# Sum over heads once per four batches, and two recurrences with gates made at eviction, a setup at the start and exponents summed by a scan

## The reference, cut to what matters

```python
# L0_attn (RWKV): k, v, r are projections; k of this reference is constant in time
#   the state's maximum pp, numerator aa and denominator bb run over 32 tokens:
#   q = max(pp, tf); e1 = exp(pp - q); e2 = exp(tf - q)
#   y = sigmoid(r) * (e1 * aa + e2 * v) / (e1 * bb + e2 + 1e-6);  out = y @ out_w.T

# L1, L2, L3 cross attention: 16 heads of depth 8, 257 keys per sequence
scores = jnp.einsum('bhqd,bhkd->bhqk', qh, kh) / sqrt(8)      # + mask or log weights
attn = softmax(scores)
out = einsum('bhqk,bhkd->bhqd', attn, vh) -> concat heads @ dense_w.T + dense_b

# L2_attn (RG-LRU)
gate_x = sigmoid(block_linear(x, ig_w, ig_b)); gate_a = sigmoid(block_linear(x, ag_w, ag_b))
log_a = -8.0 * gate_a * softplus(a_param)
a = exp(log_a); a2 = exp(2.0 * log_a)
normed_x = x * gate_x * sqrt(maximum(1.0 - a2, 1e-07))
p = cumprod(a, axis=1); p_prefix = maximum(concatenate([ones, p[:, :-1]]), 1e-07)
h = p_prefix * cumsum(normed_x / p_prefix, axis=1)
```

## Time and profile before

| | us |
|---|---|
| median of 3 runs (3683.45 to 3694.7) | 3692.14 |
| profiled execution | 3689.13 |
| its span | 3687.2 |
| busy in it: PE 2674.5, DVE 2416.8, ACT 1807.5, POOL 1662.8 | |
| first block, to the first norm | 16.2 |
| norm and recurrence of rwkv | 221.0 to 323.7 |
| norm and recurrence of rglru | 2174.3 to 2331.3 |
| cross attentions x1, x2, x3 with their norms | 808 to 1330, 1640 to 2174, 2740 to 3245 |

### The profile page before, as it was taken

How to read it: one execution, slowest core, us unless ns; L and a number is a source line. 1 busy time by engine, 2 the same in 40 slices (tenths; PEclk the granted TensorE clock), 3 DMA queues, 4 the chain that set the end, 5 groups by cost and what they waited for, 6 DMA issues and landing times. The chain is left out here.

```text
span 3687.2 us, 98216 instructions
## 1 busy us (share of the span) xinstructions
PE 2674.5 (73%) x27184; PEld 2116.8 (57%) x27185; DVE 2416.8 (66%) x8780; ACT 1807.5 (49%) x5569; POOL 1662.8 (45%) x1768
## 2 busy tenths in 40 slices
PE   5962577739999979757999970367748999978562
PEld 3741466626777669645777740256636777747552
DVE  5965711148999947646999976551148999969615
ACT  2451033328888723325888865213327777734221
POOL 2620055517777700004777740015526777736162
PEclk9975588969999979878999985559979999979665
DMA  2003043421111100201333300214434544400122
GB/s 79 1 0 96 25 118 111 117 75 40 37 37 36 28 7 0 109 0 52 72 74 72 74 25 0 55 42 116 112 87 113 110 111 111 101 1 1 35 88 69
DMA packets 209738, 224.95 MB, mean 61 GB/s; under 512 B 29651, under 2 KB 177619, under 8 KB 208948
## 3 DMA queue, kind: packets, MB, share of 16 engines
q1 hardware_dynamic: 196948, 197.56, 20.5%
q0 software_dynamic: 12672, 25.98, 2.8%
HBM read 201.68 MB, written 21.76 MB: 61 GB/s over the span
## 5 line engine op out<-in xcount | busy, mean ns | idle before, releaser
L1765 ACT ACTIVATE sx<-sx,nm 128x257 f32<-128x257 f32 x1536 | 770.5, 505 | 264.2 <-DVE nm L1809 264.2
L1680 POOL TENSOR_TENSOR sx<-sx,rs 128x1028 f32<-128x1028 f32 x384 | 731.9, 1906 | 372.0 <-DVE rs L1815 372.0
L1809 DVE CUSTOM_DVE_ANT_0 sx<-bank,rows 128x257 f32<-128x257 f32 x1024 | 393.1, 422 | 53.7 <-PE bank L1755 35.5
L247 POOL TENSOR_TENSOR rstd<-var,nhalf 128x16 f32<-128x16 f32 x24 | 69.7, 2905 | 775.3 <-DVE var L264 775.3
L1443 ACT ACTIVATE hT<-bank,B 128x128 f32<-128x128 f32 x714 | 206.0, 368 | 432.2 <-PE bank L1411 260.8
L1469 DVE TENSOR_TENSOR yb<-bank,b2s 128x128 f32<-128x128 f32 x159 | 46.4, 292 | 429.6 <-remote 230.5
L1765 ACT ACTIVATION_READ_ACCUMULATOR sx<-sx,nm 128x1 f32 x1536 | 290.3, 189 | 0.0
L1424 PE MATMUL bank<-W,hT 128*128 x1428 | 236.2, 313 | 60.6 <-ACT hT L1443 44.1
L1755 PE MATMUL bank<-kT,qb 32*128 32x257 f32 x3072 | 275.7, 428 | 6.0 <-DVE nm L1809 6.0
L1744 PE MATMUL bank<-pt,vs 128*32 128x128 f32 x6144 | 247.5, 278 | 40.1 <-ACT pt L1774 34.7
L1826 DVE COPY pt<-bank 128x512 f32<-128x512 f32 x384 | 263.6, 687 | 3.3 <-PE bank L1700 2.9
(11 more groups left out here) (391 smaller groups left out, 5924.8 us busy)
## 6 DMA issues: line engine op xcount, KB each, us to landing
ct<-in_ctxT SPq DMA_DIRECT2D x384, 128.5 KB
W<-in_L_w SPq DMA_DIRECT2D x159, 256.0 KB
rows<-rows_x SPq DMA_DIRECT2D x256, 128.5 KB
keep<-rows_keep SPq DMA_DIRECT2D x128, 128.5 KB
yg<-copy_outs SPq DMA_DIRECT2D x40, 256.0 KB
token_rows<-XN SPq DMA_DIRECT2D x24, 256.0 KB, 2.3
W<-in_L_w SPq DMA_DIRECT2D x39, 128.0 KB
wu<-in_up_w SPq DMA_DIRECT2D x1, 4608.0 KB, 14.1
```

The lines of the kernel that those rows point to most:

```text
L1680: pool.tensor_tensor(sx[:, j, :, 0:KEYS], sx[:, j, :, 0:KEYS], rs[:, j, :].unsqueeze(2).to_broadcast([P, 4, KEYS]), ALU.mult).then_inc(p_r ...
L1765: ins = act.activation(sx[:, j, h, 0:KEYS], sx[:, j, h, 0:KEYS], ACT.Exp, bias=nm[:, j, h:h + 1], scale=-1.0, accum_out=sm[:, j, h:h + 1])
L1809: dve.tensor_tensor_reduce(sx[:, j, h, 0:KEYS], B[h][:, 0:KEYS], add, -1.0, 3.0e38, ALU.add, ALU.min, nm[:, j, h:h + 1]).then_inc(s_summed ...
```

## The change

In the first block the vectors V are loaded first, with a semaphore of their own, and ACT and DVE compute there what rwkv computed at its beginning, and rglru's three scales (lru). These values live in tiles of their own (RW, decay, recur, lru). In norm, jobs named in `gates` are evicted by ACT with Sigmoid; for rglru both jobs are, and NA is 2. The loops of both recurrences are written out, and the add to X moves behind the next group's work. rglru sums the gate's values by a scan (CS, shifted by a column, set to zero where a sequence begins) and takes p and its inverse ip as two exponentials of that sum; the Exp, Ln and Exp for the root run as three passes over all groups, the last one merged with p and ip; GpSimd makes the product of gate and input. In xattn `a` has four batches in two buffers with a fifth slot for the last key's part, the sum over heads is one reduction of 4 x 32 x 5 values per four batches, and the matmul with the output weights and the add come one step later.

The core of the diff; the loops written out and the moved setup are cut:

```diff
+                sp.dma_start(V[:], T["vecs"]).then_inc(vecs_loaded.sem, 16)
...
+                st_ = Steps(act, sig, "act_step")
+                act.wait_ge(*vecs_loaded(1))
+                st_.link(act.activation(lru[:, 0:1], v("a_param"), ACT.Abs))
+                st_.link(act.activation(lru[:, 0:1], lru[:, 0:1], ACT.Exp, scale=-1.0))
+                act.activation(lru[:, 0:1], lru[:, 0:1], ACT.Ln, bias=1.0).then_inc(c_done.sem, 1)
+                act.wait_ge(*a_done(1))
...
+                dve.wait_ge(*vecs_loaded(1))
+                st_.link(dve.tensor_scalar(relu_td[:], relu_td[:], td, None, ALU.max))
...
+                st_.count(dve.tensor_copy(recur[:], ex[:, 3, :]))
+
+                st_.link(dve.tensor_copy(decay[:, :, 1:S], ex[:, 2, 0:S - 1].unsqueeze(1).to_broadcast([P, 16, S - 1])))
+
+                dve.wait_ge(*c_done(1))
+                st_.link(dve.tensor_scalar(lru[:, 3:4], lru[:, 3:4], v("a_param"), None, ALU.max))
...
-                NA = (5, 6, 5, 6)[len(jobs)]
+                NA = (5, 6, 5, 6)[len(jobs)] if len(gates) < 2 else 2
...
+                        for j in (0, 1):
...
+                                act.wait_ge(*psum[j](g + 1))
+                                act.activation(to[:, g * GW:(g + 1) * GW], B[2 + 2 * j + g % 2][:],
+                                               ACT.Sigmoid if j in gates else ACT.Identity, bias=bias).then_inc(done[j].sem, 1)
...
+                            st_.link(dve.tensor_tensor(ub[:, :, 1:S], vg[:, :, 0:S - 1], per_batch(recur[:, 0:S - 1], S - 1), ALU.mult))
...
+                            dve.tensor_tensor(y[:, q], y[:, q], RT[:, g * GW:(g + 1) * GW].rearrange("p (b s) -> p b s", s=S), ALU.mult)\
+                                .then_inc(scan_ready.sem, 1)
+                        g = k - 1
+                        if g >= 0:
+                            dve.wait_ge(*y_psum(g + 1))
+                            xg = X[:, g * GT:(g + 1) * GT, :]
+                            dve.tensor_tensor(xg, xg, B[g % 2][:].rearrange("p (t d) -> p t d", t=GT), ALU.add).then_inc(x_added.sem, 1)
...
+                        pool.tensor_tensor(GX[:, tok(g)], GX[:, tok(g)], XNT[:, tok(g)], ALU.mult).then_inc(gx_ready.sem, 1)
...
+                    for g in range(GROUPS):
+                        act.activation(A2[:, tok(g)], gate_a[:, tok(g)], ACT.Exp, scale=lru[:, 1:2]).then_inc(a2_ready.sem, 1)
...
+                        act.activation(A2[:, tok(g)], A2[:, tok(g)], ACT.Ln, scale=-1.0).then_inc(log_ready.sem, 1)
+                    act.wait_ge(*log_ready(GROUPS))
+                    for g in range(GROUPS):
+                        act.activation(A2[:, tok(g)], A2[:, tok(g)], ACT.Exp, scale=0.5).then_inc(root_ready.sem, 1)
+                        act.wait_ge(*cs_ready(g + 1))
+                        act.wait_ge(*scan_ready(g - 1))
+                        act.wait_ge(*y_psum(g - 1))
+                        act.activation(ip[:, g % 2, :], CS[:, tok(g)], ACT.Exp, scale=lru[:, 2:3])
+                        act.activation(p[:, g % 2, :], CS[:, tok(g)], ACT.Exp, scale=lru[:, 0:1]).then_inc(p_ready.sem, 1)
...
+                        dve.tensor_tensor_scan(CS[:, tok(g)], GA[:, tok(g)], keeps, 0.0, ALU.add, ALU.mult).then_inc(cs_ready.sem, 1)
+                        dve.wait_ge(*a2_ready(g + 1))
+
+                        dve.tensor_scalar(A2[:, tok(g)], A2[:, tok(g)], 1.0, -1e-7, ALU.subtract, ALU.min).then_inc(less_ready.sem, 1)
...
+                            st_.link(dve.tensor_tensor(GX[:, tok(g)], GX[:, tok(g)], A2[:, tok(g)], ALU.mult))
+                            dve.wait_ge(*p_ready(g + 1))
+
+                            st_.link(dve.scalar_tensor_tensor(out=GX[:, tok(g)], in0=ip[:, q, :], scalar=1e7, in1=GX[:, tok(g)],
+                                                              op0=ALU.min, op1=ALU.mult))
+                            st_.link(dve.tensor_tensor_scan(A2[:, tok(g)], keeps, GX[:, tok(g)], 0.0, ALU.mult, ALU.add))
+                            dve.scalar_tensor_tensor(out=p[:, q, :], in0=p[:, q, :], scalar=1e-7, in1=A2[:, tok(g)],
+                                                     op0=ALU.max, op1=ALU.mult).then_inc(scan_ready.sem, 1)
...
-                a = sb2("a", [P, 2, P])
+                a = sb2("a", [P, 2, 4, 5, S])
...
+                        if r_ % 4 == 3 and ok(x - 11):
+                            pe.wait_ge(*o_ready((x - 11) // 4 + 1 if isinstance(x, int) else i * (U // 4) + (r_ - 11) // 4 + 1))
...
+                        if r_ % 4 == 3 and ok(x - 11):
...
+                            dve.wait_ge(*a_ready(4 * (tl + 1)))
+                            dve.wait_ge(*pl_ready(tl + 1))
+                            dve.wait_ge(*y_psum(tl))
+                            dve.tensor_reduce(oT[:].rearrange("p (b s) -> p b s", b=4), a[:, tq].rearrange("p b j s -> p b s j"),
+                                              AX.X, ALU.add).then_inc(o_ready.sem, 1)
+                        b, q, tq = x - 5, (r_ - 5) % 4, (r_ - 5) % 8 // 4
...
-                            dve.wait_ge(*o_ready(4 * (tl + 1)))
-                            for k in range(4):
-                                to = oT[:, k * S:(k + 1) * S]
-                                ins = dve.scalar_tensor_tensor(out=to, in0=B[7][:, k * S:(k + 1) * S], scalar=VL[:, bass.ds(tl * 4 + k, 1)],
-                                                               in1=to, op0=ALU.mult, op1=ALU.add)
-                            ins.then_inc(pl_ready.sem, 1)
+                            dve.tensor_tensor(a[:, tq, :, 4, :], B[7][:, 0:P].rearrange("p (b s) -> p b s", b=4),
```

More of the change, by code:

```diff
@@ L208, in _ @@
                 sp.wait_ge(*loaded(2))
-        def norm(add_back=False, XN=None, fetch=None, jobs=()):
+            @block.scalar
+            def _(act):
+                st_ = Steps(act, sig, "act_step")
[4 more added lines that the diff above has]
+                act.wait_ge(*a_done(1))
+                act.activation(ex[:], ex[:], ACT.Exp).then_inc(b_done.sem, 1)
+                st_.close()
@@ L281, in _ @@
                         for j in (0, 2):
-                            if j < len(jobs):
+                            if j < len(jobs) and j not in gates:
                                 to, wt, frm, bias, scale = jobs[j]
@@ L538, in rwkv @@
                 VT, RT = sb2("VT", [P, TILES * P]), sb2("RT", [P, TILES * P])
[L539 to L546, removed]
+                norm(jobs=[(VT, w("a0_v"), XNT, v("zero"), 1.0), (RT, w("a0_r"), XNT, v("zero"), 1.0)], gates=(1,))
                 ub = sb2("ub", [P, 16, S])
@@ L608, in _ @@
-                    with st_.loop(0, GROUPS // 2, 10) as i:
-                        for q in range(2):
-                            body(i * 2 + q, q)
-                            add(i * 2 + q, q)
-                    st_.close()
-                @block.scalar
-                def _(act):
-                    act.wait_ge(*a_done(1))
-                    act.activation(ex[:], ex[:], ACT.Exp).then_inc(b_done.sem, 1)
-                    with act.Fori(0, GROUPS) as g:
-                        rg = RT[:, bass.ds(g * GW, GW)]
-                        act.activation(rg, rg, ACT.Sigmoid).then_inc(exp_ready.sem, 1)
+                    st_.link(dve.memset(ub[:, :, 0:1], 0.0))
@@ L653, in _ @@
+                @block.gpsimd
+                def _(pool):
+                    for g in range(GROUPS):
+                        pool.tensor_tensor(GX[:, tok(g)], GX[:, tok(g)], XNT[:, tok(g)], ALU.mult).then_inc(gx_ready.sem, 1)
                 @block.scalar
                 def _(act):
-                    st_ = Steps(act, sig, "act_step")
-                    st_.link(act.activation(cp[:, 0:1], v("a_param"), ACT.Abs))
-                    st_.link(act.activation(cp[:, 0:1], cp[:, 0:1], ACT.Exp, scale=-1.0))
@@ new lines, in _ @@
+                    st_.count(dve.memset(GA[:, 0:1], 0.0))
+                    st_.link(dve.memset(inner[:], 1.0))
+                    st_.link(dve.memset(inner[:, :, 0:1], 0.0))
+                    keeps = inner[:].rearrange("p b s -> p (b s)")
+                    for g in range(GROUPS):
+                        dve.tensor_tensor_scan(CS[:, tok(g)], GA[:, tok(g)], keeps, 0.0, ALU.add, ALU.mult).then_inc(cs_ready.sem, 1)
+                        dve.wait_ge(*a2_ready(g + 1))
+                        dve.tensor_scalar(A2[:, tok(g)], A2[:, tok(g)], 1.0, -1e-7, ALU.subtract, ALU.min).then_inc(less_ready.sem, 1)
```

270 lines of the change are left out of this document (111 added, 159 removed).

## The result

The changed kernel takes **3643.4 us** (median of four runs, 3639.0 to 3647.6) against 3693.4 us (3683.5 to 3698.0) for the kernel before beside it: a ratio of 0.987, 95% interval 0.984 to 0.989. It is faster by 50 us; 97 were forecast, and the time lies above the range. A second set of runs, on another chip, gave 0.987 again (0.986 to 0.989).

What follows compares the result with a forecast made beforehand. DVE's chain with waits bounds RG-LRU; cross attention has no plain bound. RWKV -24.8, RG-LRU -76.4, norms +0.5 each, start +5.5, tails +0.6, cross attention -3: -97 from 3689.1 gives 3592, plus 3.0 for the median: 3595 us, range 3560 to 3615.

Steps and rivals of the forecast that it cites:

- the work goes where there was idle time: Cross attention: the new reduction lengthens one batch of four, the others keep 3.42 us; -3 us over three stages.
- the ring DVE - ACT - DVE: Cross attention: a 3.33 us loop from reduce to next reduce, in which a reduction behind the V copy has no part.
- The bound upward (+20): Cross attention: the worst case of the -3 us term, with the reduction at 1.15 us from start to start.
- The prediction's own sign: Cross attention: the forecast is wrong if the eight-batch period leaves 28.6 us by more than 0.5.
- The price: Cross attention: the merged reduction of 640 columns takes 1.05 us, near the middle of 0.82, 1.14 (by groups) and 1.22 (by columns).
- the 4.08 of the forecast: Cross attention: length in us of the one batch in four that holds the new reduction, 4.05 - 0.30 - 0.64 + 0.97.
- hidden even at 1.5 us each: RG-LRU: GpSimd's eight products start at 0, are due from 16.6 us on, and so cost nothing.
- the forecast's 75.9 less: RG-LRU with its norm: -76.4 us for the recurrence and +0.5 us for the norm.
- the norms: Norms before the two recurrences: ACT's evictions cost one table load each, +0.5 us per norm.
- the start: First block: the moved setup waits for semaphore credits, so it ends at 21.6 instead of 16.1 us, +5.5 us.
- rivals 2 to 5: Reduction by present column cost, 3671 us (0.06); setup hidden, 3590 (0.04); alternating tables, 3636 (0.01); reduction at reciprocal's rate, 3895 (0.02).
- Rival 1: Cross attention: DVE bounds it after all, so 64 us go instead of 3; 3534 us, chance 0.12.

Runs made afterwards that it cites:

- e3: The changed kernel with the big reduction placed behind the step that makes `a`, still ahead of the reciprocal; ratio 0.982 to the kernel before.
- e4: The changed kernel with `a` laid out so that the five values of a sum lie side by side; ratio 0.979 to the kernel before.
- e7: The changed kernel with the edits of e3 and e4 together; ratio 0.971 to the kernel before.
- e6: The changed kernel with RG-LRU's eight gate products made by DVE in the norm, one behind each eviction, not by GpSimd; ratio 0.988 to the kernel before.
- f10: The changed kernel with e7's edits, e5's early credits and the gate products on DVE behind all normalized tiles; 3564.2 us, ratio 0.969 to the kernel before.
- e5: The changed kernel with SP adding the first block's six semaphore credits behind its first three DMA issues; ratio 0.987 to the kernel before, first norm at 16.38.
- f9: e1 with only the small reduction of each batch moved behind `a`; ratio 0.989 to the kernel before.
- e1: The changed kernel with the cross attention function of the kernel before; 3495.4 us against 3576.8, ratio 0.978.

## Why the prediction was wrong

**The step that failed** is the one in cross attention that says "the work goes where there was idle time; ... The other three keep 3.42". It treated the piece as if it ended with its own batch. The batch right behind it takes 3.66 us, and the other two 3.54 each: 10.74 us in place of 3 x 3.42 = 10.26. That is 0.48 us per four batches, all by which the four batches (14.82) miss the forecast's 14.34. Over 96 groups of four it would be 46 us; the three stages grew by 38.8, since the first and last batches of a stage grew less. Some of it was in the trace of before: the second long batch of the window in the earlier trace rows took 3.90 us and not 4.05, so the six others took 3.45, and their mean over the stages was 3.45 too. Against before, the batch behind is 0.30 us longer, the long one 0.08, the other two 0.08 together.

The cause of the 0.30 is shown: with `a` ahead of the same reduction (e3) the wait of the transposes' matmuls for `a` is gone and that batch takes 3.29. I had read the ring DVE - ACT - DVE and held that a step behind the V copy has no part in it. It has, through PE, by the wait for `a`, which the profile of before already showed in small (1.5 us in 7 waits). The bound upward (+20) failed with this step, because it varied only the price of the reduction and left out what is queued behind it: `a`, the transposes that need it, ACT's copy and exponentials behind these. The prediction's own sign came: the period of eight batches left 28.6 by 1.0 us.

**The price** of the reduction was a second error: 1.25 us in place of 1.05, 1.16 from start to start in place of 0.97. The reading by columns gave 1.22 and was right; the choice of a middle value was not. In e4 a reduction shorter by 0.44 made its own batch shorter by 0.47, so by an estimate from that run the 0.19 are worth some 96 x 0.2 = 19 us, not a side matter beside a miss of 42 in cross attention. That the long batch came out at the 4.08 of the forecast all the same is therefore luck: with 1.16 in its sum the forecast would have been 4.27, and what made up for the difference wasn't looked into. The price isn't the whole loss either: at 0.81 in the same place (e4) the stages are still 6.1, 4.4 and 2.9 us longer than with the old form on that chip, and only with the other order as well (e7) is four batches' time (14.18) below that of before. The small product took 0.28, not 0.20.

**RG-LRU** fell short by 6.6 us. The step "hidden even at 1.5 us each" asked only whether GpSimd's products come in time. They do; but they slow DVE down: (1.65 - 1.22) x 8 + (0.91 - 0.41) x 8 = 7.4 us, from the means of the two rows over the stage, and without them (e6, f10) the stage's loop is 7.5 us shorter. With its norm it then takes 80.7 us in f10, where the forecast's 75.9 less would be 81.4. The period (3.91) and the three table loads came as forecast.

**Right:** RWKV (5.34 us a group for 5.4), the norms, the start (22.37 for 21.6; its cause is shown by e5), and that rivals 2 to 5 would not come. Rival 1, DVE as the bound, was wrong in the other direction: DVE's work fell and the time rose.

## What to carry to other kernels

In a pipeline with no plain bound, cost a merged step by what is queued behind it in one piece, not by the sum of work, and follow each result that stands behind it to the engine that needs it; where a wait for it already shows in the profile, even a small one, expect the piece to lengthen it and the batch after. The same order that helps one form can hurt another (e3 and f9), so read who waits for what behind the piece each time. Put the operands of a reduction side by side before merging it, and look what that does to their writers. Ask of work moved to GpSimd not only whether it is done in time but what DVE runs beside it.

## What the runs showed of the hardware

- **DVE and GpSimd took turns.** GpSimd's product of 512 columns takes 1041 ns in attention; here eight take 14.04 us, 1.755 each, while DVE's scan and step grow by 1.06 and 1.0 us. Two products, a scan and a step are 2 x 1.04 + 1.22 + 0.43 = 3.73 us if nothing runs side by side, and the period was 3.55. The Trainium skill (SBUF — State Buffer, SBUF: two separate sides) says that VectorE instructions with two SBUF inputs or in a two-port mode and GpSimd's share a port pair which one of them holds for a whole instruction; this trace agrees. The same operation in the changed kernel's attention:

```profile
L470 POOL TENSOR_TENSOR kb<-KT,C 128x512 f32<-128x512 f32 x32 | 33.3, 1041 | 0.0
```

- **A step of 32 elements in the operand of a reduction** costs 0.7 ns a column (1.7 against 1.02 ns), and writing with a step of five costs 96 ns for 128 columns of `a`. The Trainium skill (SBUF — State Buffer, Door 1: The DMA port swizzle) speaks of lines of 16 bytes, and of a penalty for each access that crosses to a new one; a step of 32 or of five float32 values always crosses. That this is the cause was not tried.
- **Chips differ by stage.** On the chip of e1 to e4 the two MoE stages took 412 to 420 and 364 to 370 us, against 465 to 473 and 400 to 407 on the others; the last stage was shorter too (237 to 241 us against 253 to 257), and cross attention and the recurrences were alike within 1%. The kernel before took 3577 us there and 3679 to 3693 elsewhere. Why was not looked into.
